# Steps without expert tiles in a fused retention and mixture-of-experts kernel: group sums and zhat on ScalarE, a bank of their own for the means, four row passes moved to later steps

## The chip, the cores and the metric

One core of one Trainium2 chip. The metric is the time on the device of one launch, in microseconds. Names used: PE is TensorE (matmul), PEld its weight loads, DVE VectorE, ACT ScalarE, POOL GpSimd, SP SyncE.

## What is computed

`x` is 8 items of 512 tokens of 128 features. It is normalized to `xn`; `xn` goes through four retention blocks and, beside them, through a router with eight experts; the output joins both.

```python
def block(h, p):                      # four times, h: 8 x 512 x 128
    r = _retention(h, wk)             # causal q k^T v with row sums clipped
    m = r @ w1 + b1
    a, gate = jnp.split(m, 2, axis=-1)
    m = a * jax.nn.silu(gate) @ w2 + b2
    m = _groupnorm1(m, gg, gb)        # one mean and variance per item
    y = m + h
    f = jax.nn.gelu(y @ wf1 + bf1_, approximate=False) @ wf2 + bf2_
    return _layernorm(f + y, lg, lb)
xn = _layernorm(x); s = blocks(xn)
g = silu(expert_weight * expert_ffn[argmax(xn @ gate_w)](xn))
out = x + s * g
```

## The kernel before

**Work and order.** L = 4 layers of B = 8 items make LB = 32 work items n = 8 l + b. The program is written out by hand for each engine as a sequence of steps s = 0 to 34. Step s carries item s at its first stage (retention: products S, q, A, u), item s-1 at its second (gate and value products, SiLU, product with `w2` into bank 6, group norm), item s-2 at its third (the two GELU products, the second with the residual into bank 7) and item s-3 at its fourth (layer norm, `zhat`). `at(l, t, late, ...)` gives the item of a stage. Every engine runs its queue in order and meets the others through semaphores only.

**Expert tiles.** The 4096 tokens are sorted into 39 tiles of 128 slots. POOL scatters them by 32 indirect DMAs (L485) in steps 2 to 6; SP loads tiles from there once all 32 are in. Tile turns stand in steps 7 to 28, two in most steps (places EARLY and LATE; `turn`), so steps 0 to 6 and 29 to 34 have none. `NO_TILES` is 29. `parted` steps (9 and later, where EARLY is used) take the first GELU product as three products of split operands, `y_h` and `y_l`, with weights that POOL has split (`split_f1`, L454 and L457). In these, the second of the two first-GELU products overwrites bank 4 and so waits for DVE's copy of the transposed tile, `xtT` (L1174).

**The part around the change.**

- *Group norm of item s-1.* After the product with `w2` (L1453), DVE takes the sums by `bn_stats`, `bn_aggr` and two small instructions (L1038 to L1045), for all but items 28, 29 and 31; for these ACT takes them with two accumulating activations (`group_sums`, L663 and L664). PE spreads the sums over the partitions by a 2-column product (`means`, L1372), in bank 3 for n < 30. DVE makes the variance (L960 to L965), POOL its power -0.5 (`gn_rs`, L538), DVE scale and bias (L1123 to L1128), ACT applies them (L672), DVE adds the residual (L1136) to make `y_sb`.
- *Layer norm of item s-2, then s-3.* DVE: statistics from bank 7 (L738 to L747). POOL: power (`ln_rs`, `ln_pow`, L440). DVE: shift (`ln_nb`, L753), then two of four chunks of `zhat` (L1146); ACT in the next step the other two (L636). PE transposes `zhat` (L1322).
- *Row passes.* POOL makes the tokens of the next layer from `zhat` by a multiply with `ln_g` (L518) and an add of `ln_b` (L522), three steps after the item began.
- *Ends of steps.* In steps 2 to 6 PE runs second GELU product, `means`, transposes of u (`u_by_feature`, L1332); DVE runs `gn_moments` ahead of `split_u` (L953). In steps 29 and 30 PE runs second GELU product, transposes, `means`, and everywhere else DVE splits u first.
- *The ending.* From step 32 on DVE and POOL finish the output of all items (`silu_y`, `scale`, `norm_weights`, `centre`, `finish`). `scale(1)` (L493) stands on POOL behind the row pass of step 31.

Which semaphore counts say when the means may be written is in these lines:

```python
pe.wait_ge(gs_done, n + 1)
if n < LB - 2:
    need(pe, G_done, 2 * n)
    pe.wait_ge(gg_done, n + 1)
```

## Time and profile before

| | |
|---|---|
| median of 3 runs | 507.23 us (507.14 to 508.56) |
| the profiled execution's own time | 506.69 us |
| its span | 504.8 us |
| PE busy | 467.8 us, 93% |
| PEld busy | 390.7 us, 77% |
| DVE busy | 379.7 us, 75% |
| ACT busy | 255.0 us, 51% |
| POOL busy | 259.0 us, 51% |
| mean granted clock of PE | 0.986 of full speed |

The span is the time in the trace from the first to the last instruction; the run's own time has 1.9 us around it. Busy shares are means over all steps. Matmuls are pipelined and their ends are modelled, so the distance of two starts says more than the length of one row. A step is named here by the start of its S product (L1388): step 5 is 86.69 to 99.89 us, step 9 is 140.64 to 155.45 us, step 30 is 443.78 to 456.30 us.

### The profile page before, as it was taken

Reading aid. Unit: us, or ns where it says so; the run is one execution under the profiler, and the core shown is the slowest. Engines: PE = TensorE matmul, PEld = TensorE weight load, DVE = VectorE, ACT = ScalarE, POOL = GpSimd, SP = SyncE. Lnnn points to the kernel's source line nnn. Section 1 sums busy time; section 2 is a strip of 40 time slices with the busy share of each in tenths; the row PEclk is TensorE's granted clock in tenths of the full one; section 3 lists DMA queues with packets and bytes.
Section 4 is the critical chain, followed back from the end, with each engine's and each line's share of the span. In section 5 each row is a group of like instructions: output and inputs, shape, how many; then the busy total and the mean of one; then the engine's idle time right before and its main releaser. Section 6 shows DMA issues by size and latency. Waiting matters only on the chain. (4 is left out here: it accounts for less than half of the span.)

```text
span 504.8 us, 9878 instructions
## 1 busy us (share of the span) xinstructions
PE 467.8 (93%) x3155; PEld 390.7 (77%) x3155; DVE 379.7 (75%) x1338; ACT 255.0 (51%) x539; POOL 259.0 (51%) x287
## 2 busy tenths in 40 slices
PE   6999889999999999999999999999999999998760
PEld 5887666766889888988888898889888988765440
DVE  4768887788877767777787677777867777767997
ACT  3823334444566554565655446656554565457410
POOL 4520188888454455544545554544455556333762
PEclk9999999999999999999999999999999999999985
DMA  9899411111511111110111111111111000500014
GB/s 265 231 131 207 171 38 39 36 35 58 124 66 43 57 44 59 59 65 31 52 46 54 49 63 59 59 38 38 59 43 59 33 12 6 155 24 1 2 42 125
DMA packets 47345, 35.05 MB, mean 69 GB/s; under 512 B 13320, under 2 KB 38736, under 8 KB 47296
## 3 DMA queue, kind: packets, MB, share of 16 engines
q1 hardware_dynamic: 44496, 28.94, 22.3%
q0 software_dynamic: 2272, 4.71, 2.8%
q10 hardware_dynamic: 528, 0.79, 0.5%
q8 instruction: 27, 0.44, 0.4%
q14 instruction: 22, 0.18, 0.1%
HBM read 14.70 MB, written 9.42 MB: 48 GB/s over the span
## 5 line engine op out<-in xcount | busy, mean ns | idle before, releaser
L518 POOL TENSOR_TENSOR zhat<-zhat,all_lg 128x512 f32<-128x512 f32 x29 | 38.6, 1332 | 90.2 <-PE bank L1322 74.0
L1355 PE MATMUL bank<-all_f,G_sb 128*128 128x128 f32 x512 | 72.9, 275 | 0.0
L672 ACT ACTIVATE y_sb<-bank,gn_bi,gn_sc 128x512 f32<-128x512 f32 x32 | 24.9, 777 | 92.6 <-DVE gn_bi L1128 92.6
L1355 PEld LDWEIGHTS bank<-all_f,G_sb 128*128 128x128 f32 x512 | 67.3, 192 | 2.1 <-issue 2.0
L720 ACT ACTIVATE uT_h<-bank 128x512 fp32r<-128x512 f32 x32 | 19.1, 597 | 94.6 <-PE bank L1332 94.6
L440 POOL TENSOR_TENSOR ln_rs<-ln_ve,half_neg 128x4 f32<-128x4 f32 x32 | 33.0, 1032 | 34.6 <-DVE ln_ve L747 34.3
L1261 PEld LDWEIGHTS bank<-moe_w,h_T 128*128 128x128 f32 x312 | 39.5, 191 | 13.7 <-issue 13.7
L613 ACT ACTIVATE h_T<-bank,w_t 128x128 f32<-128x128 f32 x156 | 44.4, 371 | 5.2 <-PE bank L1277 5.2
L703 ACT ACTIVATE G_sb<-bank,all_par 128x512 f32<-128x512 f32 x64 | 42.9, 693 | 7.5 <-PE bank L1313 5.0
L568 POOL DMA_INDIRECT y_rows<-yt,slot_info x39 | 40.9, 1048 | 11.0 <-POOL yt L565 11.0
L538 POOL TENSOR_TENSOR gn_rs<-gn_ve,half_neg 128x1 f32<-128x1 f32 x32 | 18.9, 589 | 47.6 <-DVE gn_ve L965 47.5
L1277 PE MATMUL bank<-xtT,w_t 128*128 128x128 f32 x312 | 43.2, 282 | 0.0
L1023 DVE TENSOR_TENSOR rs<-pair,floor_sb 128x4 f32<-128x4 f32 x32 | 5.2, 161 | 48.8 <-PE pair L1442 48.2
L1261 PE MATMUL bank<-moe_w,h_T 128*128 x312 | 41.8, 277 | 0.0
L565 POOL TENSOR_SCALAR yt<-yt,slot_info 128x128 f32<-128x128 f32 x39 | 23.6, 606 | 30.4 <-DVE yt L1159 30.4
L522 POOL TENSOR_TENSOR htok<-zhat,all_lb 128x512 f32<-128x512 f32 x29 | 37.6, 1295 | 2.3
L1277 PEld LDWEIGHTS bank<-xtT,w_t 128*128 128x128 f32 x312 | 37.9, 192 | 0.0
L1288 PE MATMUL bank<-uT_h,all_w 128*128 128x512 f32 x64 | 35.1, 548 | 2.4 <-DVE uT_l L953 1.3
L1442 PE MATMUL pair<-S_sb,q_sb 128*128 128x129 f32 x192 | 37.1, 275 | 0.0
L485 POOL DMA_INDIRECT x_slots<-xn,pos x32 | 32.5, 1016 | 8.1 <-issue 8.1
L1411 PE MATMUL pair<-q_sb,hT 128*128 128x128 f32 x256 | 34.2, 276 | 2.5 <-ACT q_sb L656 2.4
L1353 PE MATMUL bank<-ident,y_sb 128*128 128x128 f32 x128 | 34.9, 273 | 0.8 <-ACT G_sb L703 0.8
(186 smaller groups left out, 1239.4 us busy)
## 6 DMA issues: line engine op xcount, KB each, us to landing
w_t<-moe_w SPq DMA_DIRECT2D x39, 258.0 KB
x_slots<-moe_w SPq DMA_DIRECT2D x1, 2515.5 KB, 21.3
xt<-x_slots SPq DMA_DIRECT2D x39, 64.0 KB, 1.8
x_sb<-in_L_attn_x SPq DMA_DIRECT2D x8, 256.0 KB, 5.7
moe_w<-in_L_ffn_w SPq DMA_DIRECT2D x1, 2048.0 KB, 19.8
moe_w<-y_rows SPq DMA_DIRECT2D x8, 256.0 KB, 4.6
out<-moe_w SPq DMA_DIRECT2D x7, 256.0 KB, 2.3
all_f<-in_L_attn_Wf SPq DMA_DIRECT2D x2, 512.0 KB, 5.2
```

Source lines behind the costliest of these rows:

```text
L518: pool.tensor_tensor(zhat[:, b % 2, :, :], zhat[:, b % 2, :, :], all_lg[:, li, :].unsqueeze(1).broadcast_to([P, C, D]), ALU.mult)\
L522: pool.tensor_tensor(htok[:, b * C:(b + 1) * C, 0:D], zhat[:, b % 2, :, :], all_lb[:, li, :].unsqueeze(1).broadcast_to([P, C, D]), ALU.add)\
L568: pool.indirect_dma_start(y_rows[:, :], bass.IndirectOffsetOnAxis(ap=slot_info[:, i, 0:1].bitcast(i32), axis=0), yt[ring(i)][:, :], None). ...
L613: last = act.activation(h_T[:, k * P:(k + 1) * P], bank[5][:, k * P:(k + 1) * P], ACT.Gelu, bias=w1_t[ring(i)][:, FF + k:FF + k + 1])
L703: act.activation(G_sb[:, k, :], bank[3 + k][:, :], ACT.Gelu, bias=all_par[:, w[2], F_B + k:F_B + k + 1]).then_inc(G_done, 1)
L1261: last = mm(bank[5][:, 0:D], h_T[:, k * P:(k + 1) * P], moe_w2[:, bass.ds(e, 1), k, :].rearrange("p a d -> p (a d)"), start=k == 0, stop=k ...
L1277: last = mm(bank[5][:, k * P:(k + 1) * P], w1_t[ring(i)][:, k * P:(k + 1) * P], xtT[:, :], start=True, stop=True)
L1288: mm(dst[:, :], weights[:, 0, cols], high[:, :], start=True, stop=False)
L1353: mm(dst[:, at_c], y_sb[:, n % 2, at_c], ident[:, :], start=True, stop=False, is_transpose=True)
L1355: last = mm(dst[:, at_c], G_sb[:, k, at_c], all_f2[:, li, k, :], start=False, stop=k == 1)
L1411: last = mm(pair[:, 0, at_c], hT[:, b, at_c], q_sb[:, at_c], start=True, stop=True)
L1442: last = mm(dst, q_sb[:, c * P:(c + 1) * P], S_sb[:, c - 1, :], start=False, stop=True)
```

## The change

- `SUMS_ON_ACT` names the items whose group sums ACT takes: 1 to 5, besides 28, 29 and 31 as before. DVE's four instructions for them go. `sums_by_vector` counts the others.
- `means_bank` gives bank 5 for items 2 to 5 and from 28 on (before: from 30 on), with other waits. The gate product waits for the means' copy only where the item before had its means in bank 3.
- `ZHAT_ON_ACT` names the items whose `zhat` ACT writes whole, four chunks: 0 to 3, 27 and 28. For items 0 to 3 it goes straight into `htok`, where POOL's row passes then work in place.
- The row passes of items 0 to 3 move from steps 3 to 6 to steps 7 to 10, ahead of those of items 4 to 7.
- `split_f1` for layers 1 to 3 moves from step 7 to steps 8, 9 and 10, behind `ln_pow`.
- In steps 2 to 6, PE transposes u ahead of the means, and DVE splits u ahead of `gn_moments`.

```diff
+        def means_apart(n):
+            return 2 <= n < B - 2 or n >= NO_TILES - 1
         def means_bank(n):
-            return bank[5 if n >= LB - 2 else 3]
+            return bank[5 if means_apart(n) else 3]
+        SUMS_ON_ACT = tuple(range(1, B - 2)) + (LB - 4, LB - 3, LB - 1)
+        ZHAT_ON_ACT = tuple(range(ASIDE)) + (LB - 5, LB - 4)
...
+        HTOK = [k for b in range(ASIDE) for k in (b, ASIDE + b)] + list(range(2 * ASIDE, LB))
+        def zhat_rows(n, b):
+            return htok[:, b * C:(b + 1) * C, 0:D] if n < ASIDE else zhat[:, b % 2, :, :]
...
             def step(l, t):
                 first = l == 0
                 s = l * B + t
+                if 0 <= s - (B - 1) < ASIDE:
+                    token_rows(s - (B - 1), s - (B - 1), 0)
                 w = at(l, t, 3, B, LB)
-                if w and w[0] < ENDING:
+                if w and ASIDE <= w[0] < ENDING:
...
-                if first and t == B - 1:
-                    for k in range(1, L - 1):
-                        split_f1(k)
...
-                if first and t == B - 1:
-                    split_f1(L - 1)
+                if l == 1 and t < L - 1:
+                    split_f1(t + 1)
...
-                    act.wait_ge(z_half, n + 1)
-                    for c in range(C // 2, C):
-                        last = act.activation(zhat[:, b % 2, c, :], bank[7][:, c * D:(c + 1) * D], ACT.Identity,
+                    if n in ZHAT_ON_ACT:
+                        act.wait_ge(ln_shift, n + 1)
+                        if n >= ASIDE:
+                            act.wait_ge(htok_done, htok_made(n - 2))
+                    else:
+                        act.wait_ge(z_half, halved(n + 1))
+                    for c in range(0 if n in ZHAT_ON_ACT else C // 2, C):
+                        last = act.activation(zhat_rows(n, b)[:, c, :], bank[7][:, c * D:(c + 1) * D], ACT.Identity,
...
-                if NO_TILES <= s < LB - 1:
-                    group_sums(s - 1, L - 1)
+                if s < LB and s - 1 in SUMS_ON_ACT:
+                    group_sums(s - 1, (s - 1) // B)
...
-                if w and (w[0] < NO_TILES - 1 or w[0] == LB - 2):
+                if w and w[0] not in SUMS_ON_ACT:
...
-                    for stage in (gn_moments, split_u) if first and 2 <= t < B - 1 else (split_u, gn_moments):
-                        stage(l, t)
+                    split_u(l, t)
+                    gn_moments(l, t)
...
-                    if n < LB - 2:
+                    if not means_apart(n):
                         need(pe, G_done, 2 * n)
                         pe.wait_ge(gg_done, n + 1)
...
-                    if n < LB - 1:
-                        need(pe, gn_chain, 4 * n - 3)
+                    if n and not means_apart(n - 1):
+                        pe.wait_ge(gn_chain, 4 * n - 3)
                     else:
-                        pe.wait_ge(G_done, 2 * n - 2)
+                        need(pe, G_done, 2 * n - 2)
...
-                for stage in ((gelu_second, means, u_by_feature) if first and 2 <= t < B - 1 else
-                              (gelu_second, u_by_feature, means) if s >= NO_TILES else
+                for stage in ((gelu_second, u_by_feature, means) if 2 <= s < B - 1 or s >= NO_TILES else
                               (u_by_feature, gelu_second, means)):
```

POOL, from the power of step 2 to that of step 3, before (scatters are the DMAs into `x_slots`):

```order
L440 TENSOR_TENSOR ln_rs<-ln_ve,half_neg 128x4 [waits ln_var]
L485 DMA x_slots<-xn,pos 4992x131 x4
L518 TENSOR_TENSOR zhat<-zhat,all_lg 128x512 [waits pe_zT]
L522 TENSOR_TENSOR htok<-zhat,all_lb 128x4x128 [waits hg_done]
L485 DMA x_slots<-xn,pos 4992x131 x2
L538 TENSOR_TENSOR gn_rs<-gn_ve,half_neg 128x1 [waits gn_var]
L485 DMA x_slots<-xn,pos 4992x131
L440 TENSOR_TENSOR ln_rs<-ln_ve,half_neg 128x4 [waits ln_var]
```

And in the changed program:

```order
L466 TENSOR_TENSOR ln_rs<-ln_ve,half_neg 128x4 [waits ln_var]
L511 DMA x_slots<-xn,pos 4992x131 x6
L566 TENSOR_TENSOR gn_rs<-gn_ve,half_neg 128x1 [waits gn_var]
L511 DMA x_slots<-xn,pos 4992x131
L466 TENSOR_TENSOR ln_rs<-ln_ve,half_neg 128x4 [waits ln_var]
```

The two row passes between the scatters are gone.

POOL from the power of the end of step 7 into step 9, before:

```order
L440 TENSOR_TENSOR ln_rs<-ln_ve,half_neg 128x4 [waits ln_var]
L454 CAST f_parts<-all_f 128x256
L457 TENSOR_TENSOR f_parts<-all_f,f_parts 128x256 [waits part_made]
L518 TENSOR_TENSOR zhat<-zhat,all_lg 128x512 [waits pe_zT,part_made]
L522 TENSOR_TENSOR htok<-zhat,all_lb 128x4x128 [waits hg_done]
L565 TENSOR_SCALAR yt<-yt,slot_info 128x128 [waits yt_done,info_in]
L568 DMA y_rows<-yt,slot_info 9088x128 [waits yt_weighed]
L538 TENSOR_TENSOR gn_rs<-gn_ve,half_neg 128x1 [waits gn_var]
L440 TENSOR_TENSOR ln_rs<-ln_ve,half_neg 128x4 [waits ln_var]
```

And in the changed program, where L539 and L542 are the row passes, on `htok` those of items 1 and 2:

```order
L466 TENSOR_TENSOR ln_rs<-ln_ve,half_neg 128x4 [waits ln_var]
L539 TENSOR_TENSOR htok<-htok,all_lg 128x4x128 [waits pe_zT]
L542 TENSOR_TENSOR htok<-htok,all_lb 128x4x128 [waits hg_done]
L539 TENSOR_TENSOR zhat<-zhat,all_lg 128x512 [waits pe_zT]
L542 TENSOR_TENSOR htok<-zhat,all_lb 128x4x128 [waits hg_done]
L593 TENSOR_SCALAR yt<-yt,slot_info 128x128 [waits yt_done,info_in]
L596 DMA y_rows<-yt,slot_info 9088x128 [waits yt_weighed]
L566 TENSOR_TENSOR gn_rs<-gn_ve,half_neg 128x1 [waits gn_var]
L466 TENSOR_TENSOR ln_rs<-ln_ve,half_neg 128x4 [waits ln_var]
L480 CAST f_parts<-all_f 128x256
L483 TENSOR_TENSOR f_parts<-all_f,f_parts 128x256 [waits part_made]
L539 TENSOR_TENSOR htok<-htok,all_lg 128x4x128 [waits pe_zT,part_made]
```

A row pass of an early item now follows each power directly, or behind the split of `f1`, and the split that stood behind the power of step 7 stands behind that of step 8.

PE at the end of step 3 and the start of step 4, before:

```order
L1353 MATMUL bank<-ident,y_sb 128x128
L1355 MATMUL bank<-all_f,G_sb 128x128 x2
L1372 MATMUL bank<-gs,mean_of 128x2 [waits gg_done,G_done,gs_done]
L1332 MATMUL bank<-ident,u_sb 128x128 [waits act_done,u_done]
L1332 MATMUL bank<-ident,u_sb 128x128 x3
L1388 MATMUL pair<-xn 128x129 [waits u_done]
L1388 MATMUL pair<-xn 128x129 x2
L1390 MATMUL pair<-hT,next_m 128x512
L1288 MATMUL bank<-uT_h,all_w 128x512 [waits gn_chain,uT_split]
L1289 MATMUL bank<-uT_h,all_w 128x512
```

And in the changed program:

```order
L1385 MATMUL bank<-ident,y_sb 128x128
L1387 MATMUL bank<-all_f,G_sb 128x128 x2
L1364 MATMUL bank<-ident,u_sb 128x128 [waits act_done,u_done]
L1364 MATMUL bank<-ident,u_sb 128x128 x3
L1406 MATMUL bank<-gs,mean_all 128x2 [waits slots_found,gn_chain,gs_done]
L1422 MATMUL pair<-xn 128x129 [waits u_done]
L1422 MATMUL pair<-xn 128x129 x2
L1424 MATMUL pair<-hT,next_m 128x512
L1320 MATMUL bank<-uT_h,all_w 128x512 [waits G_done,uT_split]
L1321 MATMUL bank<-uT_h,all_w 128x512
```

The transposes of u now precede the means, and the means wait for DVE's last reading of them in place of ACT's readings of bank 3.

## Rows read from the trace of the kernel before

**Rows 1.** Windows, steps 5, 9: us; busy (x) PE, PEld, DVE, ACT, POOL; clock, DMA, GB/s
```profile
86.69:99.89 13.20, 12.36 (x75) 8.97 (x73) 10.62 (x35) 5.76 (x10) 11.26 (x12) 1.00 0.11 37
140.64:155.45 14.81, 14.81 (x110) 13.20 (x109) 10.81 (x40) 8.45 (x19) 7.44 (x9) 1.00 0.18 58
```

**Rows 2.** Timeline, PE, steps 5, 6: start, us, engine, line, op, operands, count, [idle, releaser]
```profile
95.46 1.02 PE L1453 MATMUL bank<-gg_sb,all_w 128*128 128x512 f32 x2
...
99.17 0.38 PE L1372 MATMUL bank<-gs,mean_of 128*128 128x2 f32 x2 [0.47 <-DVE gs L1045]
...
106.45 0.66 PE L1322 MATMUL bank<-ident,zhat 128*128 128x128 f32 x4 [0.23 <-ACT zhat L636]
...
108.72 1.02 PE L1453 MATMUL bank<-gg_sb,all_w 128*128 128x512 f32 x2
```

**Rows 3.** Timeline, DVE and then POOL, step 6
```profile
100.04 0.15 DVE L965 TENSOR_SCALAR gn_ve<-gn_nv 128x1 f32<-128x1 f32 x1
...
101.55 0.58 POOL L538 TENSOR_TENSOR gn_rs<-gn_ve,half_neg 128x1 f32<-128x1 f32 x1
...
103.40 1.05 POOL L440 TENSOR_TENSOR ln_rs<-ln_ve,half_neg 128x4 f32<-128x4 f32 x1
```

**Rows 4.** Timelines of steps 29 and 30: PE, ACT, POOL, DVE
```profile
440.11 1.02 PE L1453 MATMUL bank<-gg_sb,all_w 128*128 128x512 f32 x2
...
442.42 0.20 ACT L664 ACTIVATION_READ_ACCUMULATOR gg_sb<-bank,all_par 128x1 f32 x1
...
445.74 0.55 POOL L538 TENSOR_TENSOR gn_rs<-gn_ve,half_neg 128x1 f32<-128x1 f32 x1 [3.27 <-DVE gn_ve L965]
...
447.69 0.69 DVE L1136 TENSOR_TENSOR y_sb<-y_sb,hT 128x512 f32<-128x512 f32 x1 [0.35 <-ACT y_sb L672]
```

**Rows 5.** Timelines, PE of step 2, POOL of step 3
```profile
54.56 1.02 PE L1453 MATMUL bank<-gg_sb,all_w 128*128 128x512 f32 x2
...
60.47 0.56 POOL L538 TENSOR_TENSOR gn_rs<-gn_ve,half_neg 128x1 f32<-128x1 f32 x1 [12.66 <-DVE gn_ve L965]
...
63.82 1.05 POOL L440 TENSOR_TENSOR ln_rs<-ln_ve,half_neg 128x4 f32<-128x4 f32 x1
```

**Rows 6.** Timelines, ACT and PE, step 8
```profile
131.21 0.81 ACT L636 ACTIVATE zhat<-bank,ln_nb,ln_rs 128x128 f32<-128x128 f32 x2
...
133.00 0.60 PE L1322 MATMUL bank<-ident,zhat 128*128 128x128 f32 x4
```

**Rows 7.** Timelines, POOL and DVE, step 8
```profile
129.93 0.39 POOL L454 CAST f_parts<-all_f 128x256 fp32r<-128x256 f32 x1
...
130.01 0.33 DVE L753 SCALAR_TENSOR_TENSOR ln_nb<-ln_mv,ln_rs 128x4 f32<-128x4 f32 x1
```

**Rows 8.** Timelines, POOL, DVE and PE, step 27
```profile
408.39 1.79 POOL L518 TENSOR_TENSOR zhat<-zhat,all_lg 128x512 f32<-128x512 f32 x1 [2.04 <-ACT zhat L636]
...
409.56 1.17 DVE L996 SCALAR_TENSOR_TENSOR gg_sb<-th_sb,gg_sb 128x512 f32<-128x512 f32 x1
...
411.08 0.47 PE L1288 MATMUL bank<-y_h,f_parts 128*128 128x512 f32 x1 [0.52 <-DVE xtT L1174]
```

**Rows 9.** Timelines, DVE and PE, step 9
```profile
146.91 0.28 DVE L1174 COPY xtT<-bank 128x128 f32<-128x128 f32 x1
...
147.56 0.39 PE L1288 MATMUL bank<-y_h,f_parts 128*128 128x512 f32 x1
```

**Rows 10.** Timelines of step 31: POOL, DVE, PE
```profile
465.64 1.27 POOL L518 TENSOR_TENSOR zhat<-zhat,all_lg 128x512 f32<-128x512 f32 x1 [3.94 <-DVE gg_sb L1006]
...
468.22 1.18 POOL L493 TENSOR_TENSOR moe_w<-moe_w,htok 128x512 f32<-128x512 f32 x1
...
462.00 0.73 DVE L1146 TENSOR_SCALAR zhat<-bank,ln_rs,ln_nb 128x128 f32<-128x128 f32 x2
...
468.25 1.16 DVE L1042 TENSOR_TENSOR gs<-gs_mv,all_par 128x1 f32<-128x1 f32 x1
...
469.72 0.38 PE L1372 MATMUL bank<-gs,mean_of 128*128 128x2 f32 x2 [0.50 <-DVE gs L1045]
```

More of the change, by code:

```diff
@@ L250, in retention_moe_kernel @@
         LAG = 3
+        ASIDE = 4
         PARTS = [("w", 0), ("f1", 0)] + [("w", l) for l in range(1, L)] + [("f1", l) for l in range(1, L)]
@@ L294, in z_bank, with sums_by_vector, halved, htok_made @@
             return bank[{LB - 2: 2, LB - 1: 5}.get(n, 7)]
+        def means_apart(n):
+            return 2 <= n < B - 2 or n >= NO_TILES - 1
         def means_bank(n):
-            return bank[5 if n >= LB - 2 else 3]
+            return bank[5 if means_apart(n) else 3]
+        SUMS_ON_ACT = tuple(range(1, B - 2)) + (LB - 4, LB - 3, LB - 1)
+        ZHAT_ON_ACT = tuple(range(ASIDE)) + (LB - 5, LB - 4)
+        def sums_by_vector(n):
+            return sum(k not in SUMS_ON_ACT for k in range(n))
+        def halved(n):
+            return sum(k not in ZHAT_ON_ACT for k in range(n))
+        HTOK = [k for b in range(ASIDE) for k in (b, ASIDE + b)] + list(range(2 * ASIDE, LB))
+        def htok_made(n):
+            return HTOK.index(n) + 1
+        def zhat_rows(n, b):
+            return htok[:, b * C:(b + 1) * C, 0:D] if n < ASIDE else zhat[:, b % 2, :, :]
         def ring(i):
@@ L1142, in z_hat @@
                     ln_shifts(n, b)
-                    need(dve, htok_done, n - 1)
+                    if n in ZHAT_ON_ACT:
+                        return
+                    if n >= ASIDE + 2:
+                        dve.wait_ge(htok_done, htok_made(n - 2))
                     dve.wait_ge(ln_shift, n + 1)
                     for c in range(C // 2):
-                        last = dve.tensor_scalar(zhat[:, b % 2, c, :], bank[7][:, c * D:(c + 1) * D],
+                        last = dve.tensor_scalar(zhat_rows(n, b)[:, c, :], bank[7][:, c * D:(c + 1) * D],
                                                  ln_rs[:, b % 2, c:c + 1], ln_nb[:, b % 2, c:c + 1], ALU.mult, ALU.add)
@@ L1321, in zhat_by_feature @@
                     for c in range(C):
-                        last = pe.transpose(bank[7][:, c * P:(c + 1) * P], zhat[:, b % 2, c, :], ident[:, :])
+                        last = pe.transpose(bank[7][:, c * P:(c + 1) * P], zhat_rows(n, b)[:, c, :], ident[:, :])
                     last.then_inc(pe_zT, 1)
@@ L1383, in step @@
                     if not first:
-                        pe.wait_ge(htok_done, n - B + 1)
+                        pe.wait_ge(htok_done, htok_made(n - B))
                         pe.wait_ge(hT_done, n - B + 1)
```

37 lines of the change are left out of this document (19 added, 18 removed).

## The prediction, as put on record before the changed kernel ran

> **What bounds the kernel now.** I read the page first: PE is busy for 93% of the span, so I asked where the other 7% lies. The windows by step answer that. In step 9, as in every step that carries expert tiles, PE is busy for 14.81 of 14.81 us: nothing can be won there, and any delay of PE is lost for good. In step 5, without tiles, it is busy for 12.36 of 13.20 us, while POOL works 11.26 us in 12 instructions [rows 1]. The modelled ends of products hide more gaps, so I measure a lap: from one product into bank 6 (L1453), called W, to the next. In steps 5 to 6 it is 108.72 - 95.46 = 13.26 us [rows 2]. Two gaps stand in it: the means product (L1372) sits 0.47 idle until DVE has the group sums, and the transposes of zhat (L1322) wait for ACT [rows 2].
>
> Then I followed what ends that lap. DVE has the variance of item 5 at 100.19, but POOL raises it to its power only at 101.55, since two row passes and two scatters stand ahead of it in POOL's queue: 1.36 us late [rows 3]. All that hangs on it (residual, zhat, S, A) is late with it.
>
> The last steps show how a lap looks with the sums on ACT, the u transposes ahead of the means and POOL without scatters. In steps 29 and 30 W is 440.11, ACT's sums end at 442.62 (W+2.51), POOL's gn_rs starts at W+5.63, and y is done at 448.38 (W+8.27) [rows 4]. The present lap has gn_rs at 101.55, W+6.09 [rows 2, 3]. The changed steps 3 to 6 have this order.
>
> **The change, part by part.** *Sums of items 1 to 5 on ACT.* DVE drops four instructions a step, ACT gains two passes and two accumulator reads, ended 2.51 after W [rows 4]. The lap of step 5 has PE's means at 99.17, W+3.71, and that lap was waiting 0.47 for DVE [rows 2], so PE comes for them at W+3.2 and, with the u transposes put ahead, at W+3.7. ACT is done 1.2 earlier and has no other work that is ready: cost 0, hidden by PE's second GELU product. If ACT were later by more, its copy of uT, next in its queue, would be late too.
>
> *Means in bank 5.* The means no longer wait for the readers of bank 3, nor the next gate product for DVE's copy of the means. Both had come already wherever sums or uT were late, so I put nothing on it alone; it is what allows DVE to split u first.
>
> *Zhat of items 0 to 3 on ACT.* ACT's two chunks take 0.81 us [rows 6], the page's shape with two overlapping instructions; at 0.49 for one, which two in 0.81 leave as a spacing of 0.32, four take 0.49 + 3 x 0.32 = 1.45.
>
> *Row passes out of steps 3 to 6.* POOL loses two passes of 1.27 us (length as in [rows 10]) and with them its delay. From gn_rs to ln_rs one scatter remains between, so ln_rs starts 1.85 after gn_rs, as at 103.40 - 101.55 [rows 3]. Hence the new lap: gn_rs at W+5.63, ln_rs from W+7.48 to W+8.53, the shift of DVE to W+8.73, four chunks on ACT to W+10.2 (ACT is free of the gate by about then: it is due at W+8.7 too), transposes at W+10.25. From there to the next W it is 2.27 now [rows 2], in which the A mask is waited for by about 0.15; it has been written earlier now, so 2.1. Lap: 12.35 instead of 13.26, a gain of 0.91, three times (the laps that end in steps 4, 5 and 6): 2.7 us. Bounds of a lap: 12.1, if ACT's zhat never decides, and 12.9, if chunks follow each other less closely and half the gain of POOL is eaten.
>
> The lap that ends in step 7 keeps DVE's half of zhat. There I take W+10.4 for the transposes and the full 2.27, so 12.7: a gain of 0.5. Step 3 begins before POOL is loaded: W of step 2 is 54.56 and gn_rs starts at 60.47, W+5.91; it would start at W+5.63, 0.28 earlier, and the scatters and ln_rs at 63.82 move with it [rows 5]. With the 0.2 that zhat on one engine saves, 0.5. **Front: -0.5 - 2.7 - 0.5 = -3.7 us.** Expert tiles do not hold it up: the 32 scatters have no pass between them and end earlier by as much.
>
> *Row passes in steps 7 to 10.* In step 7 they follow the last scatter, in PE's shadow. In steps 8, 9 and 10 the pass follows ln_rs in POOL's queue (in 9 and 10 behind the split of f1), just when DVE wants ln_rs. Step 8 shows what happens then: the cast on POOL runs 129.93 to 130.32, and DVE's shift (L753), started 0.08 later, takes 0.33 and ends at 130.34, with the cast [rows 7]. Step 27 shows it at full size: a pass holds POOL until 410.18, the gate multiply (L996) takes 1.17, and PE then sits idle for 0.52 until the copy of xtT behind it [rows 8]. In the rows, those DVE instructions wait whose inputs both lie in SBUF.
>
> The Trainium skill speaks against this move: SBUF — State Buffer, section "Who interferes with whom", says that a VectorE instruction with two SBUF inputs and a GpSimd instruction that reads SBUF exclude each other for a whole instruction, and that the order of issue decides who waits. By it the moved passes would cost something in each of the three steps, and by the rows alone the 0.52 of step 27 comes out the same way; the trace agrees.
>
> Step 8: the shift is late by 1.25 (a pass of 1.27). The slack is from ACT's end, 132.02, to the transposes at 133.00, 0.98 [rows 6]; 0.3 is left. Steps 9 and 10: the cast costs the shift 0.17 (0.33 here [rows 7]), the split of y waits some 0.2 for the first pass, the gate multiply some 0.6 for the second, so the copy of xtT is 1.0 late. It ends at 147.19 and PE needs it at 147.56 [rows 9]: 1.0 - 0.37 = 0.64 each. **Tiles: +0.3 + 0.64 + 0.64 = +1.6 us.** Bounds: nothing, if DVE gets in first or reads PSUM while a pass runs, and two whole passes (2.54) less the slack of 0.37, 2.2 a step.
>
> The splits of f1 leave step 7 and stand in steps 8 to 10; their readers come a step later. Without the 0.17 they cost nothing.
>
> *The end.* Zhat of items 27 and 28 goes to ACT whole. DVE drops two chunks (0.73 us [rows 10]) in steps 30 and 31. In step 30 PE has no gap that this closes. In step 31 the row pass waits for DVE's gate product, at 465.64; it comes 0.7 earlier, and so does the multiply behind it, that now ends at 469.40 and holds DVE's sum (L1042, 1.16 us) until 469.41. The sum is what PE's means wait for, idle 0.50 [rows 10]. Everything after hangs on DVE in one chain: **-0.65 us**, between 0 and -1.0.
>
> **Sum.** -3.7 + 1.6 - 0.65 = -2.7 us. The profiled execution took 506.69 us (span 504.8 and 1.9 around it), so it would take 504.0; the median of the runs is 0.5 higher, 507.23, so the forecast is 504.5 us. About 0.3% (1.5 us) is what a measurement of this kernel tells from no change.
>
> **Rivals.**
> - *The passes cost nothing in steps 8 to 10.* DVE gets in before the pass, or what is late is not needed. Then -3.7 - 0.65: 502.9 us. For it: in step 9 DVE is busy for only 10.81 of 14.81 us [rows 1]. Against: rows 7 and 8, where the shift and the multiply did wait. Chance 0.16.
> - *The laps do not shrink*, because another engine ends them: ACT, which in a lap now also has 1.4 us of sums (from the end of W's product, 1.02 after W, to 2.51) and 0.64 of zhat, in one queue with the gate, GELU and uT. Then the front gives only the 0.5 of step 3, and -0.5 + 1.6 - 0.65 = +0.5: 507.7 us, no change. Against: ACT is busy 5.76 of 13.20 [rows 1] and would be at 7.8 of 12.4. This is also the case in which the change does not do what it says. Chance 0.19.
> - *Slower: both passes are waited out in full in steps 8, 9 and 10.* DVE's chain runs shift, split of y, gate multiply, all with two SBUF inputs; if the first loses a whole pass and the others the second, 2.2 a step are lost, 6.6 in the three, and the total is -3.7 + 6.6 - 0.65 = +2.2: 509.5 us. It decides from 1.45 a step on, (3.7 + 0.65) / 3. This is the page's rule taken at its worst; it names no size. For it: the order of POOL's queue, the pass right behind ln_rs. Against: each wait in rows 7 and 8 was for what was left of one instruction, and S, A and zhat between read PSUM. Chance 0.09.
>
> **How the numbers follow.** The forecast has 0.56, 0.16 + 0.19 + 0.09 the rivals. The forecast's own bounds, 503.0 to 505.7, are all faster by over 0.3%, as is the first rival: faster 0.72. The second is within: same 0.19. Slower 0.09. The range takes in the first rival and the forecast whole and leaves out the slower one and the upper part of the second: 502.7 to 507.2.
>
> **What would show it.** Right: laps of 12.2 to 12.5 us that end in steps 4 to 6; gn_rs at W+5.6 with POOL idle before it; the u transposes ahead of the means, which no longer wait; the shift of DVE at over 1 us in step 8; gaps of PE before the second GELU product of steps 9 and 10 of 0.5 to 0.8, put down to the xtT copy; step 11 at 14.81 again; in step 31 L1042's successor below 0.6 us. Wrong: laps at 13 us with ACT the releaser of uT or of zhat's transposes; PE without a gap in steps 9 and 10; or steps 8 to 10 longer by 1.5 us each.

## The result, and the profile after

The changed kernel took 509.9 us (median of 8 runs, 509.63 to 511.33), beside 507.24 us (507.01 to 508.67) for the kernel before in the same session: ratio 1.005, 95% interval 1.0038 to 1.0062. Slower by 0.5%, where 504.5 us and a gain were forecast; the result lies above the range. Most kernels here, the one before too, have runs at two times some 1.6 us apart (507.0 and 508.6 for it), and as the traces have these 1.6 us behind the last w2 product (28.96 us from it to the end in before, 30.59 in e13), small differences are read from the laps.

The page of the changed kernel: span, busy times, granted clock of PE.

```profile
span 507.7 us, 9880 instructions
...
PE 467.6 (92%) x3155; PEld 391.6 (77%) x3155; DVE 369.2 (73%) x1306; ACT 265.8 (52%) x571; POOL 259.0 (51%) x287
...
PEclk9998999999999999999999999999999999999995
```

The time is not in PE's work or clock (467.6 us busy and 0.985, against 467.8 and 0.986). The windows of steps 5 and 9 answer to [rows 1]; the columns are the same.

```profile
85.90:99.55 13.65, 12.03 (x75) 8.91 (x74) 7.70 (x28) 7.79 (x16) 8.47 (x10) 1.00 0.10 34
142.78:158.13 15.35, 15.22 (x110) 13.17 (x109) 11.50 (x40) 8.54 (x19) 11.48 (x13) 1.00 0.17 57
```

POOL has 8.47 us of work in step 5 instead of 11.26, DVE 7.70 instead of 10.62, and yet the step is 0.45 us longer. Step 9 is 0.54 longer. By lap, from w2 product to w2 product (now L1487), in us; the column e16 is the same changed kernel on another chip, run e16 below:

| laps that end in step | before | after | after, e16 | forecast for the difference |
|---|---|---|---|---|
| 3 | 14.44 | 14.02 | 14.02 | -0.5 |
| 4, 5, 6 | 13.26, 13.20, 13.26 | 13.60, 13.65, 13.61 | 12.39, 12.39, 12.39 | -0.91 each |
| 7 | 13.20 | 14.92 | 13.65 | -0.5 |
| 8 | 13.08 | 12.72 | 12.73 | +0.3 |
| 9, 10 | 14.81, 14.81 | 15.36, 15.35 | 15.35, 15.34 | +0.64 each |
| 11, 12 | 14.81, 14.82 | 14.99, 15.17 | 14.98, 15.16 | 0 |
| 13 to 29 | | within 0.05 each | within 0.05 | 0 |
| 30, 31, 32 | 12.52, 13.27, 9.92 | 12.36, 13.11, 9.26 | 12.36, 13.12, 9.26 | -0.65 in all |

What is wrong with laps 4 to 6 is seen in the timelines of PE, ACT and POOL from the w2 product of step 5 on, which answer to [rows 2, 4]:

```profile
95.89 1.02 PE L1487 MATMUL bank<-gg_sb,all_w 128*128 128x512 f32 x2
...
98.97 0.60 PE L1364 MATMUL bank<-ident,u_sb 128*128 128x128 f32 x4
99.41 0.28 PE L1406 MATMUL bank<-gs,mean_all 128*128 128x2 f32 x2
...
102.21 0.50 PE L1320 MATMUL bank<-uT_h,all_w 128*128 128x512 f32 x1 [0.89 <-DVE uT_l L982]
...
98.20 0.20 ACT L697 ACTIVATION_READ_ACCUMULATOR gg_sb<-bank,all_par 128x1 f32 x1
100.84 0.60 ACT L753 ACTIVATE uT_h<-bank 128x512 fp32r<-128x512 f32 x1 [2.44 <-PE bank L1364]
...
98.63 0.96 POOL L511 DMA_INDIRECT x_slots<-xn,pos  x1 [0.30 <-issue]
102.75 0.57 POOL L566 TENSOR_TENSOR gn_rs<-gn_ve,half_neg 128x1 f32<-128x1 f32 x1 [3.17 <-DVE gn_ve L994]
```

Up to here the lap is the one that was forecast: ACT's sums are done at 98.40 (W+2.51), the u transposes start at 98.97 and the means 0.44 behind them, with no wait. But the copy uT_h, which needs the u transposes alone, starts at 100.84, 1.87 us after they do; in the part of the program that [rows 4] are from it is 0.63 (443.20 to 443.83), and in e16 0.64. ACT idles 2.44 for it, PE then 0.89 for uT_l, and gn_rs is at W+6.86, not W+5.63, with POOL idle for 3.17 before it. All behind it is the forecast's chain, 1.24 later; this delay is called the stall below. Ahead of it stand six of POOL's scatters in a row (92.24 to 99.59, one each 1.26 us): the passes that used to part them are gone. A count is what one engine or a landing DMA adds to a semaphore for another to wait for. The trace's records of the engines' counts show none between 96.93 (the w2 product) and 100.75; then four of PE's come within 0.2 us, just as the last scatter lands (100.73 to 100.99). A missing record is not yet a missing count: ACT's for the sums, due at 98.40, is not recorded at all, and PE's means, which need it, start at 99.41. But PE's are recorded, and late: second GELU product 100.75, u transposes 100.81, means 100.86, that is W+4.86, 4.92 and 4.97, where e16 has W+3.26, 3.70 and 3.82. uT_h waits for the second and starts 0.03 behind it.

### The profile page after: what moved, and what is told of

It is laid out like the page before. It is cut to its first block and busy times, and to the rows that moved or that the text cites. A ratio compares the mean times of both kernels' runs of the same rounds, so it can differ in the third digit from the quotient of the medians.

```text
span 507.7 us, 9880 instructions
## 1 busy us (share of the span) xinstructions
PE 467.6 (92%) x3155; PEld 391.6 (77%) x3155; DVE 369.2 (73%) x1306; ACT 265.8 (52%) x571; POOL 259.0 (51%) x287
## 5 line engine op out<-in xcount | busy, mean ns | idle before, releaser
L539 POOL TENSOR_TENSOR zhat<-zhat,all_lg 128x512 f32<-128x512 f32 x25 | 33.9, 1354 | 78.7 <-PE bank L1354 64.2
L1293 PEld LDWEIGHTS bank<-moe_w,h_T 128*128 128x128 f32 x312 | 39.5, 191 | 13.8 <-issue 13.8
L982 DVE TENSOR_TENSOR uT_l<-bank,uT_h 128x512 fp32r<-128x512 f32 x32 | 22.1, 691 | 19.3 <-ACT uT_h L753 19.1
L1445 PEld LDWEIGHTS pair<-q_sb,hT 128*128 128x128 f32 x256 | 31.9, 191 | 4.9 <-ACT q_sb L689 4.0
```

Source lines behind the costliest of these rows:

```text
L539: pool.tensor_tensor(z, z, all_lg[:, li, :].unsqueeze(1).broadcast_to([P, C, D]), ALU.mult)\
L1293: last = mm(bank[5][:, 0:D], h_T[:, k * P:(k + 1) * P], moe_w2[:, bass.ds(e, 1), k, :].rearrange("p a d -> p (a d)"), start=k == 0, stop=k ...
L1445: last = mm(pair[:, 0, at_c], hT[:, b, at_c], q_sb[:, at_c], start=True, stop=True)
```

## Experiments

Laps are numbered by the step in which they end. The runs were made on five chips: e1 to e4 on chip 1, e5 to e8 on chip 2, e9 to e11 on chip 3, e12 to e15 on chip 4, e16 to e18 on chip 5; the kernel before was 507.2, 507.2, 507.2, 507.25 and 507.85 us there. Each chip was used in one session only, so what is put down to the chip below may as well be something else of that session. The experiments up to e11 are told as they were read before the chips were compared.

**e1, the passes back in steps 3 to 6.**

```diff
-HTOK = [k for b in range(ASIDE) for k in (b, ASIDE + b)] + list(range(2 * ASIDE, LB))
+HTOK = list(range(LB))
-                if 0 <= s - (B - 1) < ASIDE:
-                    token_rows(s - (B - 1), s - (B - 1), 0)
+                if 0 <= s - 3 < ASIDE:
+                    token_rows(s - 3, s - 3, 0)
```

> The changed kernel with one thing undone: the row passes of items 0 to 3 run in steps 3 to 6 again, as before. All else stays changed (sums and zhat on ScalarE, means in bank 5 behind the u transposes, f1 splits in steps 8 to 10). Theory A (scatter burst): with the passes gone, six of GpSimd's scatters run back to back across the w2 product and hold up the counts that the engines post to each other; that is why ScalarE's copy uT_h starts 1.87 us after the u transposes in the laps that end in steps 4 to 6 and not 0.64 us. Then here, with the passes between the scatters, uT_h starts at W+3.7, laps 4 to 6 are 12.3 to 12.7 us, laps 7 to 10 are at or below those of before, and the whole is 502 to 504 us. Theory B (sums on ScalarE): the accumulating passes and their accumulator reads hold up ScalarE's next copy; then uT_h stays at W+4.95, laps 4 to 6 stay at 13.6, only steps 7, 9 and 10 give back their 2.8 us and about 0.7 of steps 11 and 12, and the whole is 506 to 507 us.

505.59 us, ratio 0.997 (0.9953 to 0.9983). Laps 4 to 6 are 12.96, 12.86 and 12.84, lap 7 is 13.13, and uT_h is on time. The rest of what the forecast promised a lap, 0.5, is in POOL's queue, as the later run of the same kernel (e15) shows best; DVE, then POOL:

```profile
100.08 0.15 DVE L994 TENSOR_SCALAR gn_ve<-gn_nv 128x1 f32<-128x1 f32 x1
...
95.88 1.19 POOL L539 TENSOR_TENSOR htok<-htok,all_lg 128x512 f32<-128x512 f32 x1
97.15 1.17 POOL L542 TENSOR_TENSOR htok<-htok,all_lb 128x512 f32<-128x512 f32 x1
98.48 1.01 POOL L511 DMA_INDIRECT x_slots<-xn,pos  x1 [0.15 <-issue]
99.79 0.96 POOL L511 DMA_INDIRECT x_slots<-xn,pos  x1 [0.30 <-issue]
100.78 0.58 POOL L566 TENSOR_TENSOR gn_rs<-gn_ve,half_neg 128x1 f32<-128x1 f32 x1
```

gn_ve is ready at 100.23, and two passes and two scatters hold gn_rs until 100.78. Seven scatters, each with 0.15 to 0.3 us of issue ahead of it, two passes, gn_rs and ln_rs fill POOL's lap of 12.85: in e1's window of step 5 (12.84 us) it is busy for 10.89, the other 1.95 are these issues and the short gaps between instructions, and it waits for no other engine. It is the bound here.

**e2, the sums of items 1 to 5 on VectorE again.**

```diff
-        SUMS_ON_ACT = tuple(range(1, B - 2)) + (LB - 4, LB - 3, LB - 1)
+        SUMS_ON_ACT = (LB - 4, LB - 3, LB - 1)
```

> The changed kernel with the sums of items 1 to 5 on VectorE again (all else changed, the passes moved). Theory A (scatter burst): the six scatters back to back stay, so uT_h starts at about W+4.9 as in the changed kernel, laps 4 to 6 stay at 13.6 to 13.8 us and the whole at 509.5 to 510.5 us. Theory B (sums on ScalarE are the cause): uT_h starts at W+3.7, laps 4 to 6 fall to 12.3 to 12.8 us and the whole to 506 to 507.5 us.

505.81 us, ratio 0.9971 (0.9955 to 0.9987); laps 4 to 6 are 12.38 us with the row of six scatters in place. PE, POOL, ACT in step 5:

```profile
94.36 1.02 PE L1487 MATMUL bank<-gg_sb,all_w 128*128 128x512 f32 x2
...
97.10 0.95 POOL L511 DMA_INDIRECT x_slots<-xn,pos  x1 [0.30 <-issue]
...
98.08 0.60 ACT L753 ACTIVATE uT_h<-bank 128x512 fp32r<-128x512 f32 x1 [4.01 <-PE bank L1364]
```

uT_h is at W+3.72. That looked like a verdict against the sums on ScalarE. It was none: the changed kernel had not been run on this chip.

**e3, the row of scatters parted by a wait for the means.**

```diff
+                if place == 0 and SCATTERS[t][0]:
+                    pool.wait_ge(pe_gn, t)
                 for k in range(start, start + SCATTERS[t][place]):
```

> The changed kernel with one wait more: the two scatters at the head of GpSimd's steps 3 to 6 wait for the means, so that only four run back to back and two come after the means (about W+3.9), as they do in the kernel before. Theory A (scatter burst): no hold-up, uT_h starts at W+3.7, gn_rs may wait up to 0.5 us for the second scatter, laps 4 to 6 are 12.4 to 12.9 us and the whole is 506.5 to 508 us. Theory B: uT_h stays at W+4.95, laps 4 to 6 at 13.6 or more, the whole at 509.9 us or more.

508.82 us, ratio 1.0015 (0.9999 to 1.003). Laps 4 to 6 are 13.09: uT_h is on time, but the wait costs more than was allowed for. DVE and POOL:

```profile
100.29 0.15 DVE L996 TENSOR_SCALAR gn_ve<-gn_nv 128x1 f32<-128x1 f32 x1
...
98.97 0.96 POOL L513 DMA_INDIRECT x_slots<-xn,pos  x1 [2.90 <-PE bank L1408]
100.24 0.96 POOL L513 DMA_INDIRECT x_slots<-xn,pos  x1 [0.30 <-issue]
101.23 0.57 POOL L568 TENSOR_TENSOR gn_rs<-gn_ve,half_neg 128x1 f32<-128x1 f32 x1
```

gn_ve is ready at 100.44, W+5.55, and gn_rs waits for the second scatter until 101.23, 0.8 later.

**e4, the end alone.** The front, the passes and the splits as before; zhat of items 27 and 28 on ScalarE and the means of items 28 and up in bank 5 stay.

```diff
-        ASIDE = 4
+        ASIDE = 0
-        SUMS_ON_ACT = tuple(range(1, B - 2)) + (LB - 4, LB - 3, LB - 1)
+        SUMS_ON_ACT = (LB - 4, LB - 3, LB - 1)
-            return 2 <= n < B - 2 or n >= NO_TILES - 1
+            return n >= NO_TILES - 1
```

> The kernel before with only the edits at the end: zhat of items 27 and 28 whole on ScalarE, the means of items 28 and up in bank 5. The traces put the end at 0.98 us less than before in the changed kernel. If that part stands alone, this is 506.0 to 506.5 us, 0.2% faster than the kernel before, with every lap up to step 29 as before. If the end gained only because the front had shifted something, it is 507.2 us.

506.17 us, ratio 0.998 (0.9963 to 0.9997); laps 30 to 32 are 12.36, 13.10 and 9.26, as in the changed kernel. The end's 0.98 us stands alone.

**e5 and e6, two passes of ScalarE that nobody uses, beside the row of scatters.** To e2's kernel; e6 adds accum_out to both.

```diff
+                if 2 <= s < B - 1:
+                    act.wait_ge(pe_w2, s)
+                    bias = all_par[:, 0, W2_B:W2_B + 1]
+                    act.activation(th_sb[:, :], hT[:, s - 2, :], ACT.Identity, bias=bias)
+                    act.activation(gg_sb[:, :], hT[:, s - 2, :], ACT.Square, bias=bias)
```

> The kernel of the run with the sums on VectorE (passes moved, six scatters back to back, no hold-up, laps 4 to 6 of 12.38 us, 505.8 us), with work added that nobody uses: in steps 2 to 6, once the w2 product is there, ScalarE makes two passes over 512 columns of hT (Identity and Square) without an accumulator. Theory C (any two ScalarE passes beside the scatter burst hold up the counts): uT_h starts at W+4.9, laps 4 to 7 grow by 1.24 us each, the whole is 510 to 511 us. Theory D (it takes the accumulators, or the dependence of the means on them): laps 4 to 7 stay at 12.38, 12.39, 12.38 and 13.65 us and the whole at 505.5 to 506.1 us.

> The same with an accumulator on both passes (accum_out into a tile that nobody reads). Theory D1 (the accumulator and its read are what collides with the scatters): the hold-up is back, uT_h at W+4.9, laps 4 to 7 longer by 1.24 us each, the whole 510 to 511 us, though nobody waits for these sums. Theory D2 (only the chain that runs through the sums can be held up): laps as in the run with the sums on VectorE, 505.5 to 506.3 us.

510.75 us (ratio 1.0064, 1.0047 to 1.008) and 511.64 us (1.0075, 1.005 to 1.01). Laps 4 to 6 are 13.6 to 13.7 and lap 7 is 14.92 in both. This seemed to say that any work of ScalarE calls the stall up. But the neighbours on this chip did not fit.

**e7, five scatters in a row instead of six,** in the changed kernel.

```diff
-            SCATTERS = {2: (0, 2, 4), 3: (2, 1, 4), 4: (2, 1, 4), 5: (2, 1, 4), 6: (2, 1, 2)}
+            SCATTERS = {2: (0, 2, 4), 3: (1, 2, 4), 4: (1, 2, 4), 5: (1, 2, 4), 6: (1, 2, 2)}
```

> The changed kernel (sums on ScalarE) with one of GpSimd's scatters of each step 3 to 6 moved from the head of the step to behind gn_rs: five back to back instead of six, so that the last one ends 1.26 us earlier, just before the sums do. Theory E (the hold-up ends when the last scatter of the burst has landed, about 1.15 us after it ends): the counts are free at W+3.6, the u transposes' count is not late, uT_h starts at W+3.7, laps 4 to 7 fall by 1.2 us each, the whole is 505 to 506 us. Theory F (a hold-up of fixed length follows the sums whenever a scatter runs beside them): uT_h stays at W+4.9 and the whole at 509.9 us.

511.31 us, ratio 1.0081 (1.0064 to 1.0099). Half of theory E came true: no count of an engine is recorded from 97.70 to 100.19, when the last scatter lands (100.23 to 100.42). The one at 100.19 is that of the second GELU product, W+3.52 instead of 3.26 and so late as well, but nobody waits for it then; the u transposes' own is on time (100.36, W+3.69), and so is uT_h. The time was missed all the same: the scatter that was moved stands ahead of ln_rs, which starts at W+9.12 instead of 7.50 (e16), and laps 4 to 6 are 14.02.

**e8, the passes placed elsewhere.**

```diff
+                if s == B - 2:
+                    token_rows(0, 0, 0)
...
+                if s == B - 1:
+                    token_rows(1, 1, 0)
+                if s in (B, B + 1):
+                    token_rows(s - 6, s - 6, 0, (0,))
...
+                if s in (B, B + 1):
+                    token_rows(s - 6, s - 6, 0, (1,))
+                if s in (7, 14, 21):
+                    split_f1(s // 7)
```

> A version built from what the runs show: sums of items 2 to 5 on VectorE, that of item 1 on ScalarE (lap 3 was 0.9 us shorter so), the row passes of items 0 to 3 where GpSimd has idle time and VectorE does not read two operands from SBUF: item 0 at the head of step 6 (two scatters went to steps 3 and 4 for it), item 1 in step 7 behind item 4's own passes, items 2 and 3 with their first pass behind the own passes of steps 8 and 9 and the second behind ln_rs; f1 splits in steps 7, 14 and 21. Expected: lap 3 14.0, laps 4 to 6 12.4, lap 7 12.8 to 13.2, laps 9 and 10 14.8 to 15.1, tail as in the changed kernel; 505.8 - 0.9 (lap 3) - 0.6 (lap 7) - 0.8 (laps 9, 10) - 0.3 (lap 14) = 503.2 us, 502.7 to 504.5. If the moved passes cost the same wherever they are put, 504.9 us.

511.78 us, ratio 1.0091 (1.0071 to 1.0112): a miss. One scatter more in each of steps 3 and 4 makes rows of seven, and laps 4 and 5 are 15.45 and 14.66; lap 6, with a row of six and VectorE's sums, just as in e2, is 13.67 here and 12.38 there. So ScalarE's sums are not needed for the stall. Of the placing itself, lap 7 fell to 12.70 (it has no row of six here) and lap 11 to 14.81, while laps 9 and 10 rose to 15.79: items 2 and 3 were better off before.

**e9, one lap freed of scatters,** in the changed kernel.

```diff
+            SCATTERS = {2: (0, 2, 4), 3: (2, 1, 4), 4: (2, 1, 0), 5: (0, 1, 4), 6: (2, 1, 8)}
```

> The changed kernel (sums and zhat on ScalarE) with the scatters of one lap elsewhere: none at the end of step 4 and the head of step 5 (GpSimd's steps 4, 5 and 6 have 3, 5 and 11), so that the lap from the w2 product of step 5 to that of step 6 has no scatter beside its sums, and its neighbours keep six back to back. Theory E (the burst beside ScalarE's work is the hold-up): in this lap alone uT_h starts at W+3.7 and the lap is 12.35 us, as the forecast had it for all; laps 4 and 5 stay at 13.6. If the sums on ScalarE by themselves make the lap long, it is 13.6 like its neighbours.

515.53 us, ratio 1.0146 (1.0116 to 1.0177), by lap 8, which takes 22.55 us because the tiles' loads wait for the last of eight scatters (PE idles 8.18 us for the first tile). Lap 6 is 12.33, but so, within 0.07, are laps 4 and 5 with their rows of six: 12.39 and 12.40. Up to step 4 this kernel is the changed one, and the stall is not there. Only the chip, and the session, is another.

**e10, the sum of item 1 on ScalarE, those of items 2 to 5 on VectorE** (SUMS_ON_ACT = (1, LB - 4, LB - 3, LB - 1) in the changed kernel).

> The kernel with the sums on VectorE and the passes moved (505.8 us), with the sum of item 1 alone on ScalarE, where no scatter runs. Lap 3 falls from 14.91 to 14.02 us and nothing else moves: 504.9 us (504.5 to 505.2), that is 0.996 of the kernel before. If ScalarE's work in step 2 calls up the hold-up again, laps 4 to 7 are 13.6 and the whole 509 us.

505.52 us (504.33 to 506.5), ratio 0.9942 (0.9922 to 0.9962). Lap 3 is 14.02, 0.89 less than in e2, and laps 4 to 7 stay at 12.39 and 13.66.

**e11, the passes of items 0 and 1 placed once more,** on e10. Item 0's first pass stands before gn_rs of step 6, its second at the head of step 7.

```diff
+                if s == B - 1:
+                    token_rows(0, 0, 0, (1,))
+                if s in (B + 1, B + 2):
+                    token_rows(s - 7, s - 7, 0)
...
+                if s == B - 1:
+                    token_rows(1, 1, 0)
...
                 scatter(l, t, 0)
+                if s == B - 2:
+                    token_rows(0, 0, 0, (0,))
```

> The same (sum of item 1 on ScalarE, of items 2 to 5 on VectorE, bursts of six left alone) with the passes of items 0 and 1 away from VectorE's gate multiply: item 0's first pass in step 6 before gn_rs, its second at the head of step 7, item 1's passes in step 7 behind item 4's; items 2 and 3 at the head of steps 9 and 10 as in the changed kernel; f1 splits in steps 7, 14 and 21. Expected: laps 7 and 8 together 25.9 us (26.37 before this edit), laps 9 and 10 15.2 each, lap 11 14.8: 503.6 us, 503.2 to 504.4.

508.14 us, ratio 1.0005 (0.9991 to 1.0018): a miss again. Laps 7 and 8 are 14.87 and 14.17, laps 9 and 10 15.79 each, lap 11 is 14.81 (the splits of f1 stand in steps 7, 14 and 21). POOL and DVE in step 7 (L1034 is the gate multiply), then DVE's shift and gate multiply of the lap that ends in step 9:

```profile
116.83 1.19 POOL L545 TENSOR_TENSOR htok<-htok,all_lb 128x512 f32<-128x512 f32 x1
117.96 1.27 POOL L540 TENSOR_TENSOR zhat<-zhat,all_lg 128x512 f32<-128x512 f32 x1
119.32 1.60 POOL L545 TENSOR_TENSOR htok<-zhat,all_lb 128x512 f32<-128x512 f32 x1
...
116.65 3.15 DVE L1034 SCALAR_TENSOR_TENSOR gg_sb<-th_sb,gg_sb 128x512 f32<-128x512 f32 x1
...
142.95 1.14 DVE L795 SCALAR_TENSOR_TENSOR ln_nb<-ln_mv,ln_rs 128x4 f32<-128x4 f32 x1
...
147.10 0.68 DVE L1034 SCALAR_TENSOR_TENSOR gg_sb<-th_sb,gg_sb 128x512 f32<-128x512 f32 x1
```

Three passes follow each other in POOL with less than 0.1 us between them, and the gate multiply, with both inputs in SBUF, ends at 119.80, behind two of them and the start of the third. In laps 9 and 10 the pass stands directly behind ln_rs, with no split between, and the shift waits for all of it.

**e12 to e15, the changed kernel beside three others on one chip:** the changed kernel, e2's, e5's and e1's, unaltered.

> The changed kernel itself, on the same chip as the three runs beside it. The hold-up of laps 4 to 7 was in all four kernels of one call and in none of the seven of the two others, and the calls ran on different chips. Theory G (it goes by the chip, or by something that changes from call to call, and needs the burst of six scatters only): this kernel and the three beside it agree: either all have laps 4 to 6 of 13.6 us (this one 509.9, the sums on VectorE 510.3) or none has (this one 12.4 us a lap, 505 us). Theory B (sums on ScalarE beside the burst, wherever it runs): this one has 13.6 us a lap and 509.9 us, the kernel with the sums on VectorE 12.4.

> The kernel with the sums of items 1 to 5 on VectorE again, beside the changed kernel on one chip. Theory G: it does what the changed kernel does here: both with the hold-up (510.5 us) or both without (505.8). Theory B: 505.8 us whatever the changed kernel does.

> Sums on VectorE and two passes of ScalarE beside them that nobody uses, again. Theory G: the hold-up if and only if the changed kernel has it here: 510.8 or 505.9 us. Theory C (ScalarE's work beside the burst calls it up): 510.8 us with laps 4 to 6 of 13.6 while the kernel with the sums on VectorE has 12.4.

> The changed kernel with the row passes of items 0 to 3 back in steps 3 to 6, between the scatters, again. It never has six scatters in a row. Both theories: no hold-up, laps 4 to 6 of 12.9 us, 505.6 us, on this chip too. If the chip alone makes laps longer whatever the bursts are, it is 509 us or more.

510.21 us (ratio 1.0063, 1.0045 to 1.0081), 512.17 (1.0096, 1.0077 to 1.0115), 512.2 (1.0109, 1.0089 to 1.0129) and 505.49 (0.996, 0.9948 to 0.9972). The first three have the stall in laps 4 to 7, 13.7 to 13.8 and 15.04, whoever makes the sums; e15, with the passes between the scatters, has 12.97, 12.85, 12.85 and 13.13, within 0.01 of e1 on chip 1. In e13, PE, POOL and ACT of the lap that e2 was shown for, then PE and ACT of that lap in e15:

```profile
96.97 1.02 PE L1487 MATMUL bank<-gg_sb,all_w 128*128 128x512 f32 x2
...
100.05 0.60 PE L1364 MATMUL bank<-ident,u_sb 128*128 128x128 f32 x4
...
99.70 0.96 POOL L511 DMA_INDIRECT x_slots<-xn,pos  x1 [0.30 <-issue]
...
102.07 0.60 ACT L753 ACTIVATE uT_h<-bank 128x512 fp32r<-128x512 f32 x1 [5.38 <-PE bank L1364]
...
94.68 1.02 PE L1487 MATMUL bank<-gg_sb,all_w 128*128 128x512 f32 x2
...
98.40 0.60 ACT L753 ACTIVATE uT_h<-bank 128x512 fp32r<-128x512 f32 x1 [1.21 <-PE bank L1364]
```

The same program, instruction for instruction, has uT_h at W+5.10 here and at W+3.72 there, with the last scatter of the row at W+2.73 and W+2.74; in e15, on the chip of e13 but with four in a row, uT_h is at W+3.72. Theory G holds, B and C fall.

**e16 to e18, the wait put better, and the changed kernel beside it.** e16 is the changed kernel; e17 has e3's wait, for gs_done instead of pe_gn; e18 is e17 with the sums of items 2 to 5 on VectorE.

> The changed kernel once more, on the chip of the two runs beside it, to tell whether this chip is one on which six scatters in a row hold the engines' counts up. With the hold-up: laps 4 to 6 of 13.6 to 13.8 us, 509.9 us. Without: 12.4 us a lap, 504.9 us. The theory of the burst says one of these two; both leave the kernels beside it where they are.

> The changed kernel with one wait more on GpSimd: in steps 3 to 6 the two scatters at the head of the step wait for the group sums (W+3.26), not for the means (W+3.8) as in the run that came to 508.8. So only four scatters run in a row on any chip, and the two that wait end at about W+5.6, when gn_ve is ready (W+5.5). Theory of the burst: no hold-up; laps 4 to 6 are 12.4 to 12.6 us, lap 7 is 13.7 to 13.9 (row passes beside the gate multiply), and the whole is 505 to 505.7 us, faster than the changed kernel by 0.9% wherever that has the hold-up. If a wait at any place costs 0.7 a lap as the wait for the means did, it is 507.5 to 508.

> The same wait, with the sums of items 2 to 5 on VectorE and that of item 1 on ScalarE. The group sums come at about the same time (W+3.2 to 3.3), so this is the same as the kernel beside it within 0.3 us: 505 to 505.7 us. A difference would tell what the sums on ScalarE cost by themselves.

The changed kernel took 505.57 us here (504.61 to 506.38), ratio 0.9961 (0.9937 to 0.9985); e17 504.86 (0.9952, 0.9931 to 0.9973) and e18 506.11 (0.9957, 0.9943 to 0.9971). The changed kernel is a gain of 0.4% on this chip and a loss of 0.5% in the first measurement and of 0.6% on chip 4. Its lap from step 5 on, in the same order as above, and its window of step 5:

```profile
93.34 1.02 PE L1487 MATMUL bank<-gg_sb,all_w 128*128 128x512 f32 x2
...
96.42 0.60 PE L1364 MATMUL bank<-ident,u_sb 128*128 128x128 f32 x4
96.86 0.28 PE L1406 MATMUL bank<-gs,mean_all 128*128 128x2 f32 x2
...
98.44 0.57 PE L1320 MATMUL bank<-uT_h,all_w 128*128 128x512 f32 x1
...
95.65 0.20 ACT L697 ACTIVATION_READ_ACCUMULATOR gg_sb<-bank,all_par 128x1 f32 x1
97.06 0.60 ACT L753 ACTIVATE uT_h<-bank 128x512 fp32r<-128x512 f32 x1 [1.21 <-PE bank L1364]
...
96.07 0.96 POOL L511 DMA_INDIRECT x_slots<-xn,pos  x1 [0.30 <-issue]
98.98 0.57 POOL L566 TENSOR_TENSOR gn_rs<-gn_ve,half_neg 128x1 f32<-128x1 f32 x1 [1.95 <-DVE gn_ve L994]
```

```profile
84.61:97.00 12.39, 11.76 (x75) 8.99 (x74) 7.70 (x28) 7.91 (x16) 8.48 (x10) 1.00 0.12 38
```

uT_h is at W+3.72, gn_rs at W+5.64. The wait for the sums costs nothing: laps 4 to 6 are 12.38 in e17 with rows of four and two. But chip 5 does not show the stall, so that e17 takes it away where it occurs was not tried. Who makes the sums of items 2 to 5 makes no difference to laps 4 to 7 (e17 and e18 agree within 0.01).

## Why the prediction was wrong, point by point

- **What failed.** Of the 5.4 us between forecast and result, 5.0 are one thing: in laps 4, 5, 6 and 7 uT_h starts 1.24 us late (after against e16: 13.60, 13.65, 13.61, 14.92 less 12.39, 12.39, 12.39, 13.65). The step was "Row passes out of steps 3 to 6", where POOL was said to lose "two passes of 1.27 us" and "with them its delay", and the scatters were weighed only as to when they end ("the 32 scatters have no pass between them and end earlier by as much"). What six in a row do to TensorE's counts was put at nothing. No row of before shows six in a row, since the passes always parted them; the prediction has bounds for the passes at their new place, and none for the row of scatters that they leave. Rows of six and seven have the stall and rows of five and four have no late uT_h, in kernels that ran on the same chips (e8 and e7, e12 to e14 and e15), so the row is a cause; what else the chip or the session adds to it is open.
- **The term's own size was right.** Without the stall laps 4 to 6 are 12.39; 12.35 was forecast. gn_rs came at W+5.64 (5.63), and lap 3 gave 0.42 (0.5).
- **Step 7 was mis-sized.** The passes were put "in PE's shadow". POOL, DVE and PE of the changed kernel:

```profile
121.82 1.20 POOL L539 TENSOR_TENSOR htok<-htok,all_lg 128x512 f32<-128x512 f32 x1
123.10 1.51 POOL L542 TENSOR_TENSOR htok<-htok,all_lb 128x512 f32<-128x512 f32 x1
...
121.64 1.93 DVE L1025 SCALAR_TENSOR_TENSOR gg_sb<-th_sb,gg_sb 128x512 f32<-128x512 f32 x1
...
124.42 1.13 PE L1487 MATMUL bank<-gg_sb,all_w 128*128 128x512 f32 x2 [0.81 <-DVE gg_sb L1035]
```

The pass of item 0 starts 0.18 behind the gate multiply's recorded start, the multiply takes 1.93 us instead of some 0.7 and PE waits 0.81. Lap 7 is 13.65 without the stall, not 12.7; e8 shows 12.70 with the passes elsewhere, and e9, where eight scatters hold the passes back until the multiply is done (0.68 us), 12.67. Of the 0.95, lap 8 gives 0.65 back: both together cost +0.10, against -0.2.
- **Steps 9 and 10 were right in kind and near in size.** DVE and PE, the first row from step 8:

```profile
132.07 1.14 DVE L786 SCALAR_TENSOR_TENSOR ln_nb<-ln_mv,ln_rs 128x4 f32<-128x4 f32 x1
...
148.74 1.07 DVE L1025 SCALAR_TENSOR_TENSOR gg_sb<-th_sb,gg_sb 128x512 f32<-128x512 f32 x1
149.74 0.28 DVE L1206 COPY xtT<-bank 128x128 f32<-128x128 f32 x1
...
149.64 0.40 PE L1322 MATMUL bank<-y_l,f_parts 128*128 128x512 f32 x1
150.16 0.47 PE L1320 MATMUL bank<-y_h,f_parts 128*128 128x512 f32 x1
```

The shift takes 1.14 us in step 8, the gate multiply 1.07 in step 9, the copy of xtT ends at 150.02, and PE's next product stands 0.52 behind the last instead of 0.24. Laps 9 and 10 are longer by 0.54 each (0.64). In e1, where no pass is moved, the same laps and lap 11 are 0.18 longer, and in e11, with the splits of f1 elsewhere, lap 11 is 14.81: the splits, put at nothing, cost 0.18 each, and the passes behind them 0.36 more. The two do not simply add up: in e11 the passes in laps 9 and 10 have no split ahead of them, and the laps are longer by 0.98. There the shift waits 1.14 us for the pass itself and the gate multiply runs free (0.68); in the changed kernel the shift loses only to the cast (0.33), and the multiply to the second pass (1.07). So the split ahead of the pass, 0.18 by itself, saved more than it cost. The 0.34 in lap 12 is in no term; other versions have some 0.34 in lap 14 or 19 instead, and its cause stays open.
- **The end** gave 0.98 instead of 0.65. DVE's sum is down to 0.50 from 1.16 [rows 10] and no longer what PE waits for, and lap 32 is shorter by 0.66, the forecast's 0.65; what PE still waits for there is u, as before. DVE, then PE:

```profile
471.82 0.50 DVE L1071 TENSOR_TENSOR gs<-gs_mv,all_par 128x1 f32<-128x1 f32 x1
...
471.02 0.66 PE L1364 MATMUL bank<-ident,u_sb 128*128 128x128 f32 x4 [0.53 <-DVE u_sb L1059]
```

The 0.16 of laps 30 and 31 each had been put at 0; e4 shows that they come from the end's edits; from which of them, no run shows.
- **The rivals.** That laps do not shrink came near where the stall is (in the first measurement laps 4 to 6 grow by 0.34 to 0.45), for a reason that it did not name: it is not ACT's load (7.91 of 12.39 us in e16) that ends them. That the passes cost nothing, and that both are waited out in full, fell. The last of these has 509.5 us, near the 509.9 that were measured, but by luck: its 2.2 us a step in steps 8 to 10 are 0.54 in laps 9 and 10, and lap 8 is shorter. On chip 5 the sum of the differences is -2.2 us of span (502.6 against 504.8), where -2.7 was forecast, and the profiled run took 504.61 us.

## What to carry to other kernels

When work is moved out of an engine's queue, look at what it used to keep apart, not only at what it delayed: the row passes cost 2.5 us of POOL a lap and were also what kept a row of scatters at four. A suspected cause is told from a chance companion only by kernels that run on the same chip, in the same session, as the one that shows the effect; two theories about ScalarE looked proven here until the changed kernel ran beside them. Where a gain needs a long row of indirect DMAs, keep the version that was fast on every chip it ran on, as e1 (0.997 and 0.996), or part the row with a wait that falls into the queue's idle time, as in e17, which cost nothing without the stall and was not tried where the stall occurs.
